# Draining attention fills one step later: ScalarE, GpSimd and VectorE work of a macaron block on one Trainium2 core

## What is computed

```
x = x + 0.5 * ffn(layernorm(x));  x = x + attn(layernorm(x));  x = x + 0.5 * ffn(layernorm(x))
ffn(x)  = (silu(x @ wg.T) * (x @ wu.T)) @ wd.T          # 256 -> 768 -> 256, integer weights / 127
attn(x): q, k, v = x @ Wq.T, x @ Wk.T, x @ Wv.T          # 16 heads of 16 channels
         scores = q @ k.T / 4 - slope[head] * |i - j|
         out = softmax(scores) @ v @ Wo.T + bo
```

## Time and profile before

| | |
|---|---|
| runs | 867.07, 868.13, 871.92 us (median 868.13) |
| profiled execution | 870.15 us, span 868.4 us |
| mean granted TensorE clock | 0.977 |
| attention | 198.4 us (first scores) to about 711 us |
| HBM traffic | 12.02 MB read, 4.62 MB written |

### The profile page before, as it was taken

One profiled execution on the slowest core, in us unless ns is written; L12 is line 12 of the kernel. 1 busy time (PEld: TensorE's weight loads), 2 busy tenths in 40 slices (PEclk: granted clock), 3 DMA queues, 4 the chain that ended last, 5 costly groups with the idle time before them and its releaser, 6 DMA issues.

```text
span 868.4 us, 13024 instructions
## 1 busy us (share of the span) xinstructions
PE 803.4 (93%) x4576; PEld 490.8 (57%) x4576; DVE 645.6 (74%) x1347; ACT 518.4 (60%) x745; POOL 429.6 (49%) x486
## 2 busy tenths in 40 slices
PE   2699999998899999999999999999898989999997
PEld 2578887864344444444444444444453438888886
DVE  5488877767887777877777777777878717777764
ACT  4334444336678678677678678678577674434443
POOL 0343345344446646646546646546545544444433
PEclk9799999999899999999999999999899999999999
DMA  9230025303550551451451451351441000000001
GB/s 366 111 41 3 2 34 79 40 2 47 68 72 18 62 72 22 57 74 24 52 73 23 56 76 26 50 75 23 52 56 20 2 3 27 26 26 27 26 26 50
DMA packets 21491, 43.18 MB, mean 50 GB/s; under 512 B 3848, under 2 KB 5912, under 8 KB 21208
## 3 DMA queue, kind: packets, MB, share of 16 engines
q1 hardware_dynamic: 21400, 41.92, 28.2%
HBM read 12.02 MB, written 4.62 MB: 19 GB/s over the span
## 4 chain that ended last, share of the span: by engine, by line
PE 63%; DVE 24%; DMA 4%; issue 3%; POOL 2%; SPq 2%; ACT 1%; DVEq 0%; ACTq 0%
PE ps L948 60%; DVE row_max L817 13%; DVE hid L752 3%; DMA q_aug<-max_row 2%; DMA q_scale<-q_scale 2%; PE ps L960 1%; DVE max_in L827 1%; DVE newton L684 1%; PE ps L1006 1%; DVE max_in L829 1%; DVE rstd L686 1%; POOL x_sb L503 1%; POOL probs L520 1%; DVE xnt L873 1%; SPq L361 1%
## 5 line engine op out<-in xcount | busy, mean ns | idle before, releaser
L817 DVE TENSOR_REDUCE row_max<-ps 128x1 f32<-128x512 f32 x512 | 329.0, 684 | 110.8 <-PE ps L948 110.0
L640 ACT ACTIVATE probs<-ps 128x1024 f32<-128x1024 f32 x256 | 260.1, 1026 | 49.7 <-PE ps L948 49.2
L520 POOL TENSOR_TENSOR probs<-probs,diag 128x256 f32<-128x256 f32 x256 | 190.7, 748 | 180.6 <-ACT probs L640 180.2
L452 POOL TENSOR_TENSOR hid_r<-hid,hid_r 128x512 fp32r<-128x512 f32 x96 | 124.7, 1301 | 189.5 <-ACT hid_r L547 188.5
L948 PE MATMUL ps<-xnt,wgu_r 128*128 128x512 f32 x768 | 193.9, 406 | 17.3 <-DVE hid L752 13.0
L948 PEld LDWEIGHTS ps<-xnt,wgu_r 128*128 128x128 f32 x768 | 144.6, 192 | 58.1 <-DVE hid L752 18.1
L948 PE MATMUL ps<-k_aug,q_aug 60*128 60x512 f32 x512 | 152.9, 435 | 15.2 <-DVE row_max L817 9.8
L948 PE MATMUL ps<-probs,v_aug 128*32 128x512 f32 x1024 | 141.3, 625 | 7.3 <-POOL probs L520 7.3
L553 ACT ACTIVATE gated<-ps 128x512 f32<-128x512 f32 x96 | 57.3, 598 | 131.3 <-PE ps L948 122.1
L948 PE MATMUL ps<-q_aug,k_aug 62*128 62x512 f32 x512 | 129.5, 501 | 2.9 <-DMA q_aug<-max_row 2.4
L948 PEld LDWEIGHTS ps<-q_aug,k_aug 62*128 62x128 f32 x512 | 48.5, 186 | 114.4 <-issue 69.6
(11 more groups left out here) (72 smaller groups left out, 656.4 us busy)
## 6 DMA issues: line engine op xcount, KB each, us to landing
q_aug<-parts SPq DMA_DIRECT2D x96, 128.0 KB, 4.3
k_aug<-parts SPq DMA_DIRECT2D x96, 128.0 KB, 5.9
x_sb<-x_in SPq DMA_DIRECT2D x8, 512.0 KB, 12.7
x_out<-x_sb SPq DMA_DIRECT2D x8, 512.0 KB, 2.7
diag<-diag_table SPq DMA_DIRECT2D x1, 2048.0 KB, 18.8
wgu_i<-w_gate_up SPq DMA_DIRECT2D x2, 768.0 KB, 6.1
w_att<-w_att SPq DMA_DIRECT2D x1, 1024.0 KB, 11.3
q_aug<-max_row SPq DMA_DIRECT2D x64, 8.0 KB
```

Of the source, the lines that this page charges most:

```text
L452: nc.gpsimd.tensor_tensor(hid_r[:, 1, f, :], hid[:, f % 2, :], hid_r[:, 0, f, :].bitcast(F32), ALU.subtract).then_inc(s["hid_lo"], 1)
L520: nc.gpsimd.tensor_tensor(tile, tile, diag[:, kt % 2, n * QH + 2 * pair:n * QH + 2 * pair + 2, :], ALU.mult).then_inc(fixed, 1)
L640: nc.scalar.activation(probs[:, kt % 2, 2 * pair:2 * pair + 2, :], ps[:, at:at + 2, :], ACT.Exp, scale=SLOPE_UNITS[pair]).then_inc(exp_don ...
L817: nc.vector.reduce_max(row_max[:, quad % 2, u % 2, u // STEPS, (u % STEPS) // 2:(u % STEPS) // 2 + 1], max_bank(tile), mybir.AxisListType. ...
```

## The change

ScalarE no longer drains the fill of a step behind that step's exponential. Fills stand at even steps (and the maxima at step 5); the drain of an even step's fill now comes behind the exponential of the odd step that follows, and at step 5 the heads' drain comes ahead of that of the maxima. GpSimd's part of a fill comes one fix later, VectorE's part one pair of reductions later. TensorE's and SP's orders are the same as before. One line is added, so line numbers behind it are one higher.

```diff
 # GpSimd, turn(b)
-                        name = FILLS.get((n, s))
+                        name = FILLS.get((n, s - 1))
                         if name in fills_of(b):
                             take(b, name)
 # ScalarE, turn(b), behind the exponential
-                        name = FILLS.get((n, s))
-                        if name in fills_of(b):
-                            drain(b, name)
+                        if s % 2 == 1:
+                            for name in (FILLS.get((n, s - 1)), FILLS.get((n, s))):
+                                if name in fills_of(b):
+                                    drain(b, name)
 # VectorE, turn(b), behind row_maxima of the step
-                        name = FILLS.get((n, s - 1))
+                        name = FILLS.get((n, s - 2))
                         if name in fills_of(b) and name.startswith(HEADS):
                             divide(b, name)
                         if name in fills_of(b) and name.startswith(SPLIT_DVE):
                             split(b, name)
```

## The result

The changed kernel takes **902.51 us** (median of 4 runs, 899.76 to 902.77), the kernel before 870.02 us on the same chip (4 runs, 867.07 to 872.37): a ratio of **1.037, 95% interval 1.033 to 1.040**. The prediction was 879.3 us, range 869.0 to 884.5. The direction holds; the size does not, by a factor of three. The profiled executions differ by 901.0 - 868.4 = 32.6 us of span, and all of it lies in the attention stage, which lasts from the first to the last exponential 543.3 us in place of 510.8.

What follows compares the result with a forecast made beforehand. The prediction took TensorE (busy 93%, 60% of the chain), with VectorE's row maxima and the maxima's DMA, as the bound. Terms 7.7 + 2.8 + 0 + 0.7 = +11.2 us on 868.13 gave 879.3 us, range 869.0 to 884.5.

Steps and rivals of the forecast that it cites:

- DMA term: Sequence ends: qk transfers issued later delay the first maxima's DMA, 1.1 us each, +7.7 us (4.9 to 9.5) over seven.
- quad 0: VectorE's lo part of xt0 is held behind GpSimd's fix of (0, 2): +0.4 us in seven sequences, +2.8 us.
- quad 1: Gains and a possible VectorE-GpSimd collision at turn1's lo part, -3.0 to +2.4 us over five sequences; taken as 0, the middle.
- heads ahead of the maxima: Step 5: TensorE's transpose of the maxima waits for the later heads' drain, late once in the last sequence: +0.7 us.
- the sum: 7.7 + 2.8 + 0 + 0.7 = +11.2 us, added to the median of 868.13 us.
- The queue, the port and their places: Maxima's DMA queues behind qk transfers, SP 1.36 us later; VectorE and GpSimd exclude each other in quads 0 and 1.
- TensorE waits for it: At (0, 0), scores stand behind the maxima's second transfer, the last 0.30 us with nothing to do.
- Seven times 1.1: Later maxima transfers delay the scores of (0, 0) by 1.1 us at seven sequence ends: +7.7 us.
- Rival A: The maxima's transfers do not wait for the qk transfers, so that cost is zero: 871.6 us, chance 0.17.
- rival B: Negation at (1, 3) runs free, 0.4 instead of 2.0 us in five sequences, queue has room: 860.8 us, chance 0.07.
- I work out 0.58 us of the 0.72 as gained: At (1, 3), TensorE's 0.72 us wait shrinks because qk1's lo part moves behind the fix of (1, 1).
- The work that follows has two steps of room, so I take this gain as nothing: Odd steps' exponentials start sooner, but this was priced at zero except at (1, 3).

Runs made afterwards that it cites:

- run 5: Kernel before, with only the qk2 and qk3 pieces moved behind the next step's exponential: 887.5 us, ratio 1.017 to the kernel before.
- run 12: Kernel before, with only the quad 0 fills that go through VectorE alone (xt0, xt1, heads3) moved: 873.2 us, ratio 1.002 to the kernel before.
- run 1: Changed kernel, with qk2 and qk3 drained behind their own step's exponential again: 878.6 us, ratio 1.012 to the kernel before.
- run 3: Changed kernel, with six unused products filling TensorE's wait for the first maxima at (0, 0) of sequences 1 to 7: 886.4 us, ratio 1.018 to the kernel before.
- run 10: Changed kernel, with SP sending qk3 and qk1 rows behind the maxima and VectorE's normalisations moved to quads 2 and 3: 849.9 us, ratio 0.976 to the kernel before.
- run 11: Kernel before, with SP sending qk3 and qk1 rows behind the maxima and VectorE's normalisations moved to quads 2 and 3: 855.5 us, ratio 0.983.
- run 9: Changed kernel, with SP sending the qk3 and qk1 rows behind the maxima instead of ahead: 876.9 us, ratio 1.008 to the kernel before.
- run 8: Changed kernel, with VectorE's four normalisations moved from quad 1 to quads 2 and 3: 880.9 us, ratio 1.013 to the kernel before.
- run 4: Changed kernel, with unused products filling both TensorE waits, six at (0, 0) and seven at (1, 5): 883.2 us, ratio 1.015 to the kernel before.
- run 6: Kernel before, with three unused products in each of the two quad 1 waits, at (1, 3) and (1, 5): 862.6 us, ratio 0.992.

## Why the prediction was wrong in size

| step | forecast us | measured us |
|---|---|---|
| DMA term, a sequence | 1.1 | 1.3 (9.0 us over seven ends), 1.4 (run 5, sequence 4) |
| quad 0, a sequence | 0.4 | 0.4 (run 12, sequence 4) |
| quad 1, a sequence | 0 (-0.6 to +0.5) | +0.1, +0.3 (run 1, sequences 2 and 5, steps against sequences 2 and 4 before) |
| heads ahead of the maxima, last sequence | 0.7 | 0.6 |
| clock, whole kernel | not in the sum | about 19 (estimate) |

- *The queue, the port and their places* were right, with numbers close to the forecast: SP 1.38 us later, the second transfer 3.94 us, the lo part of xt0 1.20 us in run 12, and in the last sequence the transpose of the maxima late once, behind the heads' drain:

```profile
729.72 0.28 PE L1007 MATMUL ps<-eye,max_in 128*32 128x128 f32 x1 [0.60 <-ACT stage L598]
```

In the changed kernel itself xt0's lo part takes 1.19 to 1.23 us in sequences 1 and 7 alone, and 0.75 in sequences 2 to 6.

- *Quad 1 at the middle* came out nearly right, as the sum of two parts: 0.6 to 0.8 us gained at (1, 3), as worked out there, and about 1 us lost at (1, 5), where the port went the bad way in each of sequences 1 to 5.
- Without a stretch at 1.2 GHz, sequences with all of the change take 66.2 to 66.3 us (run 3) against 64.1 to 64.6: about 1.9. The end of the stage gains 1.3 (below), and 7 x 1.9 + 0.6 - 1.3 = 13 us stands against the 11.2 of the sum.
- **The step that failed** is "TensorE waits for it", priced as "Seven times 1.1" and summed with terms of the same kind: it prices a wait of TensorE at the length of the wait. The clock's share is, as an estimate, (72 - 24) x 0.4 = about 19 us, and 13 + 19 = 32 is close to the difference of the spans, 32.6. (The profile has it as 11 us of waits and 22 us of busy time; that a wait gets shorter where TensorE is slow ahead of it is argued, not shown.) The sum had no term for it and the text no word, though the row of the clock in the page of before has two eights in the attention stage, and stretches of a microsecond show five there, all of them at a wait of quad 1.
- *Rival A* (room in the queue) needed a transfer of 2.8 us or less and fell; *rival B* needed the negation in under 0.5 us, and it takes 1.30 (1.96 before); the port took that gain back.
- "I work out 0.58 us of the 0.72 as gained" was right, and the later costs hid it: run 10 against run 11 shows 0.56 to 0.84 us at (1, 3) of sequences 1 to 5.
- "The work that follows has two steps of room, so I take this gain as nothing" held within the sequences, where run 10 against run 11 shows about 0.1 us behind (1, 3). It did not hold at the end of the stage, where no step follows: TensorE's last wait for a fix falls from 2.25 to 0.93 us, in the changed kernel too.

What stays open is which waits draw a stretch at 1.2 GHz: 12 of 12 from 1.4 us on in the changed kernel, 6 of 6 in run 9, 5 of 7 in run 5, 4 of 6 in run 1, but 3 of 11 in run 8. Before the change a pair of 0.72 and 0.82 us drew one in some sequences and none in others. That filling them removes the stretches (runs 3, 4 and 6) is shown; a rule for a single wait is not.

## What to carry to other kernels

On an engine that is busy nine tenths of the time, read the row of the granted clock before pricing an idle gap: here a wait of 1.5 to 1.8 us cost itself and, in the changed kernel, about another 1.4 or 2.7 us of slow products behind it. A change of order that looks bad may be a good one that meets a queue and a port: name the transfer or instruction that it collides with and move that, then compare both orders again. Filling a suspected wait with unused products separates the price of the wait from that of the clock in one run, if the steps of sequences without a stretch stay as they were; in run 6 they did not quite.

## What the hardware showed that was not expected

- Added work made a kernel faster: six unused products a sequence, in waits of 0.7 and 0.8 us, took 0.8% off the kernel before (run 6, about half of it by the clock), and six in a wait of about 1.5 us took 16 us off the changed one (run 3).
- The stretches at 1.2 GHz are 3.4 or 6.8 us long nearly everywhere (one of 17, one of 14 and two of 10 us aside). In the changed kernel those of sequences 1 to 7 begin at the end of a wait or within 3 us behind it, and the one shown goes on while TensorE is busy without a gap. A us of them costs the changed kernel about 0.4 us.
- Equal idle time does not mean equal clock: 32 us of waits in the stage went with 72 us at 1.2 GHz in the changed kernel, and with 24 us in run 8.
- Two instructions of VectorE and GpSimd that start within 0.01 us of each other cost 1.0 us (0.40 to 1.42) in each of five sequences of the changed kernel. VectorE lost each time, though by the record it had begun first in four of the five.
